# Graph layer on one core: rows fetched one by one for a quarter group in each third round instead of each sixth, in loops of three rounds

## What is computed

```python
h = jnp.maximum(_layernorm(x, axis=-1), 0.0)
cat = jnp.concatenate((h[src], h[dst], edge_attr_128), axis=-1)   # 200000 x 384
msg = jax.nn.relu(cat @ W1 + b1)
aggr = jax.ops.segment_sum(msg, dst, num_segments=12500)
x = x + layernorm(aggr + h) * gamma + beta
```

## Time and profile before

| what | value |
|---|---|
| median of 3 runs | 2849.47 us (2840.32 to 2862.66) |
| span of the profiled execution, first to last instruction | 1949.5 us |
| the rest of the profiled execution's own time | not given by the profile |
| mean granted TensorE clock over the span | 0.899 |
| gathers by POOL in the main loop | 1484 |
| rows fetched by hand | 1024 by SP, 1024 by ACT |

### The profile page before, as it was taken

One profiled execution on the slowest core, in us unless ns is written; L12 is line 12 of the kernel. 1 busy time (PEld: TensorE's weight loads), 2 busy tenths in 40 slices (PEclk: granted clock), 3 DMA queues, 4 the chain that ended last, 5 costly groups with the idle time before them and its releaser, 6 DMA issues.

```text
span 1949.5 us, 52908 instructions
## 1 busy us (share of the span) xinstructions
PE 1548.5 (79%) x11881; PEld 1483.7 (76%) x11881; DVE 1256.9 (64%) x3454; ACT 659.4 (34%) x1507; POOL 1463.9 (75%) x1559
## 2 busy tenths in 40 slices
PE   5688788778878787877787788787788888877887
PEld 5678788777777777877777787777777877777786
DVE  7656666667666666666666676666566665656665
ACT  5533333333333333333333333333323232322323
POOL 7777777777777777777777777777777777777776
PEclk9888888989889998998989998999898888888988
DMA  9755656556565655656565565656556565555554
GB/s 261 204 143 144 167 143 166 152 156 166 144 169 145 164 152 155 163 147 169 149 160 153 155 166 144 168 140 168 147 154 163 138 164 148 155 148 153 163 145 106
DMA packets 229468, 306.84 MB, mean 157 GB/s; under 512 B 46461, under 2 KB 141157, under 8 KB 229317
## 3 DMA queue, kind: packets, MB, share of 16 engines
q1 hardware_dynamic: 151858, 192.55, 34.4%
q0 software_dynamic: 49536, 101.55, 21.4%
q10 hardware_dynamic: 27922, 11.43, 2.7%
HBM read 281.72 MB, written 23.64 MB: 157 GB/s over the span
## 4 chain that ended last, share of the span: by engine, by line
issue 22%; DMA 22%; POOL 20%; PE 13%; DVE 10%; DVEq 8%; ACT 2%; ACTq 2%; POOLq 1%; SPq 0%
DMA a_rows<-table_a,picks 20%; POOL a_rows L613 19%; DVEq L1398 5%; DVE onehot_cols L1367 3%; PE ps_pre L769 3%; PE ps_pre L770 3%; PE ps_sum L781 2%; DVE msg L1387 2%; PE ps_edge L756 2%; PE ps_fin L781 1%; DVE aggr L1408 1%; ACTq L1027 1%; DMA table_a<-a_out 1%; DVEq L1383 1%; PE ps_sum L788 1%
## 5 line engine op out<-in xcount | busy, mean ns | idle before, releaser
L613 POOL DMA_INDIRECT a_rows<-table_a,picks x1484 | 1401.8, 945 | 452.4 <-issue 400.3
L769 PE MATMUL ps_pre<-w_c,edge_cols 128*128 128x128 f32 x3128 | 671.5, 300 | 29.5 <-issue 29.2
L770 PE MATMUL ps_pre<-b_win,onehot_cols 128*128 128x128 f32 x3128 | 663.2, 297 | 0.0
L995 ACT ACTIVATE msg<-msg 128x512 f32<-128x512 f32 x390 | 245.7, 630 | 951.9 <-DVE msg L1387 893.1
L769 PEld LDWEIGHTS ps_pre<-w_c,edge_cols 128*128 128x128 f32 x3128 | 537.1, 215 | 38.6 <-issue 37.0
L1387 DVE TENSOR_TENSOR msg<-ps_pre,a_rows 128x512 f32<-128x512 f32 x374 | 257.0, 687 | 433.8 <-DMA a_rows<-table_a,picks 339.4
L770 PEld LDWEIGHTS ps_pre<-b_win,onehot_cols 128*128 128x128 f32 x3128 | 534.7, 214 | 0.0
L1367 DVE SCALAR_TENSOR_TENSOR onehot_cols<-space,base_all,ps_hot 64x512 f32<-64x512 int32 x391 | 438.3, 1121 | 0.6 <-DMA space<-in_dst 0.6
L781 PE MATMUL ps_sum<-onehot,msg 128*128 128x64 f32 x1560 | 214.6, 283 | 105.2 <-ACT e_rows L1013 71.3
L781 PEld LDWEIGHTS ps_sum<-onehot,msg 128*128 128x128 f32 x1560 | 200.5, 201 | 123.4 <-ACT e_rows L1013 82.2
L991 ACT ACTIVATE edge_cols<-ps_edge 128x512 f32<-128x512 f32 x391 | 228.4, 584 | 136.8 <-PE ps_edge L756 115.7
(11 more groups left out here) (137 smaller groups left out, 1073.8 us busy)
## 6 DMA issues: line engine op xcount, KB each, us to landing
edges<-in_edge_attr SPq DMA_DIRECT2D x195, 512.0 KB
space<-in_dst SPq DMA_DIRECT2D x195, 256.0 KB
a_rows<-table_a,picks POOLq DMA_INDIRECT x1484
hand_rows<-table_a SPq DMA_DIRECT2D x1024, 0.5 KB
hand_rows<-table_a ACTq DMA_DIRECT2D x1024, 0.5 KB
b_win<-table_b SPq DMA_DIRECT2D x391, 32.0 KB
table_b<-b_rows ACTq DMA_DIRECT2D x96, 64.0 KB
out<-out_rows SPq DMA_DIRECT2D x96, 64.0 KB
```

The lines of the kernel that those rows point to most:

```text
L613: pool.indirect_dma_start(a_rows[:, u, k, :], None, table_a[:, :], bass.IndirectOffsetOnAxis(ap=picks[:, u, k:k + 1], axis=0),).then_inc(s ...
L769: pe.matmul(to, edge_cols[:, u % 2, k * P:(k + 1) * P], w_c[:, :], start=True, stop=False)
L770: mm = pe.matmul(to, onehot_cols[:, u % 2, k * P:(k + 1) * P], b_win[:, u, :], start=False, stop=True)
L995: act.activation(msg[:, u % 2, :, :], msg[:, u % 2, :, :], ACT.Relu).then_inc(s_msg, 1)
```

## The change

- `PERIOD` goes from 6 to 3: quarter 3 of group u = 0 is fetched by hand in each third round, so `HANDS` goes from 16 to 32, and POOL issues three gathers instead of four there.
- SP issues 72 of the 128 rows (nine batches of 8, at places given by `SLOTS`) and ACT 56 (`ACT_ROWS`, seven batches of 8 instead of sixteen of 4). ACT's batches stand at the end of a group, behind the relu; before, they stood between `columns` and the relu.
- The row numbers are stored 16 places apart (`PLACE`), 8 used, so that one TENSOR_LOAD reads numbers that begin at a multiple of 64 bytes. SP reads the receivers' numbers of three rounds (12) in one load from `base_sp`; DVE reads those of a round (4) at its start from `base_dve`.
- SP, ACT, POOL and DVE loop over three rounds. SP waits once for two windows.
- One semaphore counts the quarters of a slot (`s_a_rows[u]`); by-hand rows have three (`s_hand_sp` twice, `s_hand_act`). `early_columns` goes ahead of `columns` on ACT.

```diff
-PERIOD = 6
+PERIOD = 3
 BATCH = 8
+PLACE = 16
-ACT_ROWS = 64
+ACT_ROWS = 56
+FIRST_BATCHES = 5
...
+        def load_bases(engine, bases, at, n):
+            _, values = nc.values_load_multi_w_load_instructions(
+                bases[0:1, bass.ds(at, n)], [engine], min_val=0, max_val=N - 1,
...
+            return values
...
-                def window(i, u, base):
-                    if u == 0:
+                def windows(i, h, base, end=PAIR):
+                    if h == 0:
                         sp.wait_ge(s_b_stored, 16 if isinstance(i, int) and i < 2 else (i - 1) * 16)
                         sp.sem_inc(s_gate_sp, 1)
                     if past(i, 1):
-                        sp.wait_ge(s_pre, (i - 1) * UNROLL + u + 1)
+                        sp.wait_ge(s_pre, (i - 1) * UNROLL + h * PAIR + end)
...
+                SLOTS = ((None, 0, 1, 2), (3, 4, 5, None), (6, 7, 8, None))
+                def rounds(t):
+                    base = load_bases(mybir.EngineType.SP, base_sp, t * PLACE, PERIOD * UNROLL)
+                    for j in range(PERIOD):
+                        round_(t * PERIOD + j, base[j * UNROLL:(j + 1) * UNROLL], t, SLOTS[j])
...
                 with sp.Fori(1, EARLY_GROUPS) as s:
-                    rounds(s)
+                    with sp.Fori(0, 2) as n:
+                        rounds(s * 2 + n)
+                    load_early(s)
...
+                def hand_round(i, groups):
+                    for u in range(groups):
+                        step(i, u, HAND_K if u == 0 else SUB)
                 def rounds(s):
-                    for n in range(EARLY // PERIOD):
+                    for n in range(2):
                         with pool.Fori(n * PERIOD, (n + 1) * PERIOD - 1) as j:
                             for u in range(UNROLL):
                                 step(s * EARLY + j, u)
...
+                        hand_round(s * EARLY + (n + 1) * PERIOD - 1, UNROLL - n)
...
                     for u in range(groups):
+                        if u == 3 and early:
+                            early_columns(i)
                         if not (last and u == groups - 1):
                             columns(*after(i, u, 1))
-                        if t is not None and j * UNROLL + u < len(ACT_SLOTS) and ACT_SLOTS[j * UNROLL + u]:
-                            fetch(t, par, j * UNROLL + u)
...
                             relu(i, u)
...
+                        for batch in slots[u]:
+                            fetch(t, batch)
...
+                NEXT, SLOTS = ((), (), (0,), ()), (((1,), (), (2,), (3,)), ((4,), (), (5,), (6,)))
...
+                        dve.wait_ge(s_hand_sp[0], handed * (FIRST_BATCHES * BATCH * 16))
+                        dve.wait_ge(s_hand_sp[1], handed * ((SP_ROWS - FIRST_BATCHES * BATCH) * 16))
+                        dve.wait_ge(s_hand_act, handed * (ACT_ROWS * 16))
...
-                def base_of(g):
-                    return dve.value_load(base_i[0:1, bass.ds(g, 1)], min_val=0, max_val=N - 1)
...
+                    base = load_bases(mybir.EngineType.DVE, base_dve, i * UNROLL, UNROLL)
```

More of the change, by code:

```diff
@@ L499, in load_early, with fetch @@
                                  ).then_inc(s_early_loaded, 16)
-                def fetch(t, par, batch):
+                def fetch(t, batch):
                     if batch == 0 and past(t, 1):
-                        sp.wait_ge(s_z, ((t - 1) * PERIOD + PERIOD - 1) * UNROLL + 1)
+                        sp.wait_ge(s_z, hand_used(t))
                         sp.sem_inc(s_gate_sp, 1)
[L506 to L518, removed]
+                    numbers = hand_numbers(mybir.EngineType.SP, t, batch)
+                    for p in range(BATCH):
+                        sp.dma_start(hand_row(batch * BATCH + p), row_at(numbers[p])
+                                     ).then_inc(s_hand_sp[0 if batch < FIRST_BATCHES else 1], 16)
@@ new lines, in round_ @@
+                def round_(i, base, t=None, slots=(None,) * 4):
+                    pair(i, 0)
+                    if slots[0] is not None:
+                        fetch(t, slots[0])
+                    windows(i, 0, base)
+                    if slots[1] is not None:
+                        fetch(t, slots[1])
+                    pair(i, 1)
+                    if slots[2] is not None:
+                        fetch(t, slots[2])
+                    windows(i, 1, base)
+                    if slots[3] is not None:
+                        fetch(t, slots[3])
@@ L535, in _ @@
                 rounds(0)
+                rounds(1)
+                load_early(0)
                 with sp.Fori(1, EARLY_GROUPS) as s:
[L537 to L539 removed]
+                    with sp.Fori(0, 2) as n:
+                        rounds(s * 2 + n)
+                    load_early(s)
+                base = load_bases(mybir.EngineType.SP, base_sp, HANDS * PLACE, 2 * UNROLL)
+                round_(ROUNDS - 2, base[0:UNROLL])
                 pair(ROUNDS - 1, 0)
[L541 to L544, removed]
+                windows(ROUNDS - 1, 0, base[UNROLL:])
+                tail()
+                windows(ROUNDS - 1, 1, base[UNROLL:], LEFT - PAIR)
                 for b in range(ROUNDS - 4, BLOCKS - 1):
@@ new lines, in hand_round, with rounds @@
+                def hand_round(s, n, early):
+                    loaded = s + n if not isinstance(s, int) or s + n > 0 else None
+                    round_(s * EARLY + n * PERIOD + PERIOD - 1,
+                           (None, s * (EARLY - 1) + n * (PERIOD - 1) + PERIOD), early=early, handed=s * 2 + n + 1,
+                           loaded=loaded)
+                def rounds(s, n, early):
+                    with dve.Fori(0, PERIOD - 1) as j:
+                        plain_round(s, n, j, early)
+                    hand_round(s, n, early)
@@ new lines, in _ @@
+                for j in range(PERIOD - 1):
+                    plain_round(0, 0, j, True)
+                hand_round(0, 0, True)
+                rounds(0, 1, True)
+                half = EARLY_ROWS // EARLY
+                with dve.Fori(1, half) as s:
+                    with dve.Fori(0, 2) as n:
+                        rounds(s, n, True)
+                rounds(half, 0, True)
+                for j in range(PERIOD - 1):
+                    plain_round(half, 1, j, PERIOD + j < EARLY_REST)
```

202 lines of the change are left out of this document (107 added, 95 removed).

## The result

The kernel after takes 3016.4 us (median of 4 runs, 3009.87 to 3022.73), the kernel before 2844.89 us on the same occasions (4 runs, 2825.61 to 2862.66). The ratio is 1.061, with an interval of 1.056 to 1.067: slower by 6%, where the forecast was 2829.5 us and the range ended at 2860.

The account below looks back on a forecast made before the run. POOL's gathers were taken to pace the main loop at 1.2495 us each. 16 fewer give 20.0 us, all other terms nothing, the 900 us outside the span untouched: 2849.5 - 20.0 = 2829.5 us, range 2806 to 2860 us.

Parts of the forecast that it names:

- I take it as a part that the change does not touch.: The 900 us between profiled span and median time were taken to stay as they are, leaving 2829.5 us.
- the first rival: The 900 us grow and shrink with the span, so the time falls in proportion to 2820.2 us; chance 0.20.
- POOL is the pacer: In the main loop POOL's gathers, 1.2495 us each, set the pace; PE, DVE and ACT fit in beside it.
- the -20.0 us: On POOL, 16 gathers fewer at 1.2495 us each were to take 20.0 us off span and time.
- The second rival: TensorE at 1.2 GHz throughout makes PE the bound, 2011 us; saved gathers gain nothing, time stays 2849 us; chance 0.20.
- I take 49.4 us of 56.2, 88%: SP's work in three rounds, 49.4 us, was to stay under the 56.2 us of POOL's 45 gathers, costing nothing.
- the third rival: By-hand rows on SP or ACT become the pacer, slower: 2877.5 us at 3.0 us beyond POOL's room; chance 0.10.
- at the low end of its 525 to 977 ns: On SP, loads of aligned row numbers were to be faster than the median 761 ns, saving 9 x 0.23 = 2.1 us.
- If the shorter body turns without that stop: SP's loop turn costs up to 3.7 us, putting SP at 95%; without that cost it stays at 88%.
- It fits ... So: nothing: ACT's eight-row batches, 25 us in three rounds beside some 20 us busy, and their place behind the relu cost nothing.
- late by -0.4 to +3.5 us: By-hand rows reach DVE's addition (L1452) this late, 1.5 us taken; POOL's 6.0 us of room was to cover it.
- the signs of being wrong: POOL waits for L1452 or `pick`; second, SP's waits shrink while PE waits for `edges` or `b_win`; span falls, time does not.

Follow-up runs that it names:

- e0: The kernel before, unchanged, profiled once more: 2780.02 us, with a span of 2778.2 us.
- e10: The kernel after with a quarter in each sixth round only, loops of six rounds again: 2895.24 us, 1.014 of before.
- e6: The kernel after with SP's row loads replaced by plain semaphore increments, the 16 of each batch in a loop of eight turns: 3070.07 us (one run).
- e4: The kernel after with SP's 72 rows of each by-hand quarter left out, ACT's 56 kept: 2850.85 us (two runs), 1.011 of before.
- e9: The kernel after with ACT's batches of eight ahead of the relu again, all 4096 rows issued: 3043.33 us, 1.067 of before.
- e1: The kernel after without by-hand rows, POOL gathering every quarter: 2748.46 us, 0.963 of before.
- e3: The kernel before without its by-hand rows, POOL gathering every quarter: 2746.87 us, 0.973 of before.
- e8: The kernel after without by-hand rows, each SP batch replaced by one DMA of eight neighbouring rows, unused: 2738.96 us, 0.971 of before.

## Why the prediction was wrong, step by step

**The step that failed first: "I take it as a part that the change does not touch."** The 900 us between the profiled span and the median were inside the execution, as the first rival said; e0 has less than 2 us outside. The Trainium skill (Runtime: NRT & Kernel Launch, section "The ~15µs preamble/postamble breakdown") had spoken against that step with its 9 to 15 us; the trace agrees that nothing large lies around the kernel, with under 2 us here. The rival's own price failed all the same: the time did not grow and shrink in proportion, since what the 900 us consist of is not spread over all work. What the traces show of them are stops in queues, waits for these, and matmuls at a lower clock (e0).

**"POOL is the pacer"** held for the execution read and not for e0, whose span fits the timed ones. In e0 POOL waits 831 us for `picks`, so the -20.0 us were worth nothing. The second rival had this, but with TensorE's lower clock as the reason and "no gain" as the result. The clock is lower in e0, 0.775, yet PE is busy for only 66% of the span, so it is not the bound that the rival made it.

**SP's sum, "I take 49.4 us of 56.2, 88%".** Measured: 87.6 us. The pieces were right as medians and as code; what was missing are the stops and pauses. A batch stood at 2.5 us and takes 2.2 to 8.0 in the turn shown, 4.5 on the mean of all 288. 32 turns of 87.6 us are 2803 us, and 144 us ahead of them and 63 behind (2947.3 to the end of the span, 3010.2) make up the whole time. That is the third rival's mechanism, by-hand rows as the pacer, which had a chance of 0.10: right in place and sign, its price too small, since it was worked out from the earlier trace rows and counted only what exceeds the room of a POOL that does not pace.

**The register loads: "at the low end of its 525 to 977 ns".** The opposite. One view of the line that reads row numbers, for both queues, answers to the earlier trace rows:

```profile
L369 SPq TENSOR_LOAD <-hand_picks x288: 2/902/1181, 143.6 to 2944.0; - x144
...
L369 ACTq TENSOR_LOAD <-hand_picks x224: 16/740/1026, 163.5 to 2938.9; - x112
```

The median on SP went from 761 ns (706 in e0) to 902 ns, and ACT's load of eight takes 740 where its load of four took 492. The 12 numbers in one load are 919 ns on SP, inside the bounds (0.3 to 1.71) and above the 0.57 taken. What alignment by itself did was not tried.

**The loop turn.** "If the shorter body turns without that stop": it does. From the last DMA of a turn to the next pair are 2.40 us (1008.65 to 1011.05, with a load of 0.92 in it) where the earlier trace rows have 5.10. The rule of the Trainium skill (Runtime: NRT & Kernel Launch, section "Instruction fetch mechanics") agrees: the trace after has 31 packets on the instruction queue, e0 142 and e10, with its loops of six rounds, 146. It saved some 2.7 us in each two turns, which take 175 us, and was not felt. That rule fits the turns and not the stops, which stand in e6's loop of four instructions too.

**ACT: "It fits ... So: nothing".** Wrong for the rows: ACT's 1792 cost 102 us (e4). Right for the place: behind the relu is no dearer than ahead of it (e9).

**The new wait: "late by -0.4 to +3.5 us".** The addition of hand rows idles longer; the view of that tile, what its engine waited for, and how often:

```profile
L1452 DVE TENSOR_TENSOR msg<-ps_pre,hand_rows x32: 282/292/293, 218.8 to 2948.7; 128x128 f32<-128x128 f32 x32
its engine sat idle before it (us, times) until:
  DMA hand_rows<-table_a: 107.5, 31
```

107.5 us in 31 times is 3.5 us each, the upper end as a mean, and up to 8.9. The 6.0 us of POOL's room that were to cover it are not there, since POOL itself waits 1001 us for `picks`, which DVE makes behind that addition.

**DVE's register loads, semaphores, `early_columns`, windows: nothing.** Right to some 1%: e1 and e3 lie 2 us apart by their times, 1% by their ratios. Of the signs of being wrong the second came true: SP's own waits shrink to 57 us, and PE waits for `edges`, where e0 has 74.6 us:

```profile
PE ps_edge L791 <- DMA edges<-in_edge_attr: 210.2, 69, 10.6
```

## What to carry to other kernels

Before any sum is made from a profile, hold its span against the time to be explained; where they differ by more than a few us, profile again, since medians may agree to the nanosecond while the time of a queue is made by its slow tail. Price an issuing queue by the time from its first to its last instruction divided by the turns, not by the sum of typical durations. Work handed from one engine to another's queue in many small instructions can be dear even where that engine is 22% busy, as ACT is here: a row by hand cost some 40 to 80 ns of end time, by the runs that are compared, and one DMA for eight rows cost nothing.

## What was not expected of the hardware

- Stops of about 700 ns in instructions that wait for nothing. They came on SP (276 of 2304 MOVEs at L519), on ACT (79 of 1792 at L1061), and on POOL as soon as it had quick instructions (508 of 4488). They are not the reading of new code (e6), and packets of the same number cost no time (e8). They are no fault of one chip: e0 to e10 ran on five. What does bring them, and why the execution of 1949.5 us has none, stays open. One rival was not tried: every timed run has a span and a granted clock on record, so the profiler recorded each while it was timed, and the queues may be stopping for that recording. Against it, the execution of 1949.5 us was recorded too; whether in the same way is not known.
- Without by-hand rows the kernel still stands at 2748 us with PE and DVE at the head of the chain (e1). PE pauses there as well: 343 of its matmuls start over 500 ns after the one before them though they wait for nothing, 390 us together; in the execution of 1949.5 us none does. What the time would be without these pauses was not tried.
- Padded row numbers that begin at multiples of 64 bytes were read in 902 ns on SP, against 761 ns (706 in e0) in the packed layout; on DVE four numbers in one load took 345 ns, against 305 for one.
